# Two gathers in flight, each begun on the landing of the last but one, in both edge walks of a graph layer with routed experts

## The reference, cut to what matters

```
# graph attention, 8 heads of 32
q, k, v = x @ Wq + bq, x @ Wk + bk, x @ Wv + bv
logits  = einsum('ehd,ehd->eh', q[dst], k[src]) / sqrt(32)
expv    = exp(logits - segment_max(logits, dst)[dst])
attn    = expv / segment_sum(expv, dst)[dst]
agg     = segment_sum(attn * v[src], dst)
y       = x + gelu(agg + x @ Wskip + bskip);  layernorm(y) * gamma + beta

# routed experts: a second small attention (4 heads of 4) over 131072 edges
h       = x @ W_gat;  e = leaky_relu(a_src[src] + a_dst[dst]);  alpha = softmax of e per dst
scores  = mean over heads of layernorm(segment_sum(h[src] * alpha, dst) + b_gat)
out     = sum over 4 experts of gate * (gelu(x @ W1 + b1) @ W2 + b2)     # top 2 of 4 by scores
```

## Time and profile before

| | us |
|---|---|
| median of 3 runs | 4069.05 (4067.04 to 4070.93) |
| span of the profiled execution | 5874.6 |
| first to last gather of attention | 339.6 to 3494.4 |
| first to last gather of routing | 3740.4 to 5692.5 |
| GpSimd busy | 2589.4 |
| VectorE busy | 3464.7 |
| TensorE busy with matmuls | 3912.2 |
| GpSimd waiting for the message step (attention) | 1232.4 |
| GpSimd waiting for a free routing slot | 675.7 |

### The profile page before, as it was taken

One profiled execution on the slowest core, in us unless ns is written; L12 is line 12 of the kernel. 1 busy time (PEld: TensorE's weight loads), 2 busy tenths in 40 slices (PEclk: granted clock), 3 DMA queues, 4 the chain that ended last, 5 costly groups with the idle time before them and its releaser, 6 DMA issues. The chain is left out here.

```text
span 5874.6 us, 106076 instructions
## 1 busy us (share of the span) xinstructions
PE 3912.2 (67%) x26108; PEld 2753.9 (47%) x26109; DVE 3464.7 (59%) x9273; ACT 2543.2 (43%) x6305; POOL 2589.4 (44%) x2723
## 2 busy tenths in 40 slices
PE   7857777777777777777777773355666666666550
PEld 3335555555555556555555563233434343443330
DVE  8856666666666666666666668434444444444348
ACT  4445555555555555554555555223333333333320
POOL 3244444444444444444445441444444444445540
PEclk9978888888888888888888885577877787777765
DMA  6455555555555555555556555111111111111117
GB/s 212 147 163 165 155 168 163 163 161 168 156 159 163 161 168 156 165 158 165 154 166 172 159 150 177 44 15 18 21 19 21 19 21 19 22 18 19 20 21 263
DMA packets 367690, 683.50 MB, mean 116 GB/s; under 512 B 70294, under 2 KB 240482, under 8 KB 367074
## 3 DMA queue, kind: packets, MB, share of 16 engines
q0 software_dynamic: 157888, 427.05, 27.9%
q1 hardware_dynamic: 183106, 223.68, 11.5%
q10 hardware_dynamic: 26080, 25.70, 1.5%
HBM read 588.41 MB, written 87.78 MB: 115 GB/s over the span
## 5 line engine op out<-in xcount | busy, mean ns | idle before, releaser
L746 POOL DMA_INDIRECT KV<-kv_d,src_i x1564 | 1482.7, 948 | 1677.7 <-DVE msg L839 1232.4
L1389 POOL DMA_INDIRECT re_src<-src_tab_d,rsrc x1024 | 974.5, 952 | 978.7 <-SPq L1399 675.7
L1013 PE MATMUL agg_ps<-msg,oh 128*128 128x264 f32 x3512 | 1085.8, 455 | 229.7 <-issue 218.4
L1013 PEld LDWEIGHTS agg_ps<-msg,oh 128*128 128x128 f32 x3512 | 744.4, 222 | 414.2 <-issue 282.7
L1597 PE MATMUL ex_y_ps<-ex_w,ex_hid 128*112 128x256 f32 x1792 | 586.6, 461 | 301.6 <-issue 299.1
L966 PE MATMUL Q<-q,ohT 128*128 128x256 bf16 x5328 | 753.0, 297 | 15.6 <-issue 13.9
L839 DVE TENSOR_TENSOR msg<-KV,weigh_ps 128x1056 f32<-128x1056 f32 x439 | 545.7, 1243 | 268.6 <-ACT weigh_ps L920 250.1
L1516 ACT COPY re_ohT<-re_ohT_ps 128x1024 bf16<-128x1024 bf16 x179 | 181.0, 1011 | 1075.0 <-remote 1010.6
L966 PEld LDWEIGHTS Q<-q,ohT 128*128 128x128 bf16 x5328 | 531.4, 105 | 117.4 <-issue 19.5
L909 ACT ACTIVATE square<-iota_b,off 128x128 bf16<-128x128 bf16 x1784 | 569.2, 392 | 0.3
L1597 PEld LDWEIGHTS ex_y_ps<-ex_w,ex_hid 128*112 128x112 f32 x1792 | 363.7, 214 | 434.1 <-issue 366.0
(11 more groups left out here) (264 smaller groups left out, 6199.0 us busy)
## 6 DMA issues: line engine op xcount, KB each, us to landing
q<-q_d SPq DMA_DIRECT2D x446, 192.0 KB
y_d<-ex_y ACTq DMA_DIRECT2D x56, 448.0 KB
rg_ye<-y_d SPq DMA_DIRECT2D x7, 3584.0 KB, 11.8
KV<-kv_d,src_i POOLq DMA_INDIRECT x1564
nu_xs<-xs_d SPq DMA_DIRECT2D x7, 2688.0 KB, 11.9
re_src<-src_tab_d,rsrc POOLq DMA_INDIRECT x1024
kv_d<-pr_kv SPq DMA_DIRECT2D x49, 260.0 KB, 2.2
xs_d<-pr_xs SPq DMA_DIRECT2D x49, 256.0 KB, 2.4
```

The costliest lines, as they stand in the source:

```text
L746: pool.indirect_dma_start(out=KV[:, t % (KVR * G), :], out_offset=None, in_=k.kv_d, in_offset=bass.IndirectOffsetOnAxis(ap=k.src_i[:, t:t ...
L1013: m = pe.matmul(agg_ps[:, 0:HEADS * HW], oh32[ring(s, 2)][:, t, :], msg[ring(s, 2)][:, t, :, :].rearrange("p h e -> p (h e)"), start=False ...
L1389: pool.indirect_dma_start(out=gs[:, t % (RING * RG), :], out_offset=None, in_=k.src_tab_d, in_offset=bass.IndirectOffsetOnAxis(ap=k.rsrc[: ...
```

## The change

Both walks now hold at most two gathers in flight: before gather t, GpSimd waits for the landing of gather t-2 (`FLY = 2`). Semaphores count by tile in place of group or half group. A group's tiles are announced when its last gather has landed. In the routing walk GpSimd makes this announcement, and SyncE keeps only the release of slots. What else is computed and moved stays as it was.

```diff
+FLY = 2
 ...
 # attend
-        kv_landed = [nc.alloc_semaphore(f"at_kv_landed{i}") for i in range(4)]
+        kv_landed = [nc.alloc_semaphore(f"at_kv_landed{i}") for i in range(G)]
 ...
-                def landed(n):
-                    pool.wait_ge(kv_landed[n % 4], 16 * G * (n // 4 + 1))
-                    pool.sem_inc(ok["tiles"], G)
+                def landed(t):
+                    pool.wait_ge(kv_landed[t % G], 16 * (t // G + 1))
+                    if t % G == G - 1:
+                        pool.sem_inc(ok["tiles"], G)
 ...
                     for t in range(n * G, (n + 1) * G):
+                        if t >= FLY:
+                            landed(t - FLY)
                         pool.indirect_dma_start(...)
-                                                ).then_inc(kv_landed[n % 4], 16)
-                    if n:
-                        landed(n - 1)
-                landed(NG - 1)
+                                                ).then_inc(kv_landed[t % G], 16)
+                for t in range(NT - FLY, NT):
+                    landed(t)
 ...
 # route_experts
+                def landed(t):
+                    pool.wait_ge(gathered[t % 4], 16 * (t // 4 + 1))
+                    if t % RG == RG - 1:
+                        pool.sem_inc(ok["tiles"], RG)
                 for n in range(RNG):
                     if n >= RING:
                         pool.wait_ge(ok["used"], n - RING + 1)
-                    for half in range(2):
-                        h = 2 * n + half
-                        if n:
-                            pool.wait_ge(gathered[(h - 2) % 4], 16 * (RG // 2) * ((h - 2) // 4 + 1))
-                            pool.sem_inc(ok["ring_seen"], 1)
-                        for t in range(n * RG + half * (RG // 2), n * RG + (half + 1) * (RG // 2)):
-                            pool.indirect_dma_start(...).then_inc(gathered[h % 4], 16)
+                    for t in range(n * RG, (n + 1) * RG):
+                        if t >= FLY:
+                            landed(t - FLY)
+                        pool.indirect_dma_start(...).then_inc(gathered[t % 4], 16)
+                for t in range(RT - FLY, RT):
+                    landed(t)
 ...
             def _(sp):
-                for n in range(RNG):
-                    if RING <= n + RLEAD < RNG:
-                        old = n + RLEAD - RING
-                        end = sp.value_load(k.rlast_tab[0:1, old:old + 1], min_val=1, max_val=RSTEPS)
-                        sp.wait_ge(ok["val"], end)
-                        sp.sem_inc(ok["used"], 1)
-                    for h in (2 * n, 2 * n + 1):
-                        sp.wait_ge(gathered[h % 4], 16 * (RG // 2) * (h // 4 + 1))
-                    sp.sem_inc(ok["tiles"], RG)
+                for n in range(RING, RNG):
+                    end = sp.value_load(k.rlast_tab[0:1, n - RING:n - RING + 1], min_val=1, max_val=RSTEPS)
+                    sp.wait_ge(ok["val"], end)
+                    sp.sem_inc(ok["used"], 1)
```

More of the change, by code:

```diff
@@ L1382, in _ @@
                         pool.wait_ge(ok["used"], n - RING + 1)
-                    for half in range(2):
-                        h = 2 * n + half
-                        if n:
-                            pool.wait_ge(gathered[(h - 2) % 4], 16 * (RG // 2) * ((h - 2) // 4 + 1))
-                            pool.sem_inc(ok["ring_seen"], 1)
-                        for t in range(n * RG + half * (RG // 2), n * RG + (half + 1) * (RG // 2)):
-                            pool.indirect_dma_start(out=gs[:, t % (RING * RG), :], out_offset=None, in_=k.src_tab_d,
-                                                    in_offset=bass.IndirectOffsetOnAxis(ap=k.rsrc[:, t:t + 1], axis=0)).then_inc(gathered[h % 4], 16)
+                    for t in range(n * RG, (n + 1) * RG):
+                        if t >= FLY:
+                            landed(t - FLY)
+                        pool.indirect_dma_start(out=gs[:, t % (RING * RG), :], out_offset=None, in_=k.src_tab_d,
+                                                in_offset=bass.IndirectOffsetOnAxis(ap=k.rsrc[:, t:t + 1], axis=0)).then_inc(gathered[t % 4], 16)
+                for t in range(RT - FLY, RT):
+                    landed(t)
             @block.sync
             def _(sp):
-                for n in range(RNG):
-                    if RING <= n + RLEAD < RNG:
-                        old = n + RLEAD - RING
-                        end = sp.value_load(k.rlast_tab[0:1, old:old + 1], min_val=1, max_val=RSTEPS)
-                        sp.wait_ge(ok["val"], end)
-                        sp.sem_inc(ok["used"], 1)
-                    for h in (2 * n, 2 * n + 1):
-                        sp.wait_ge(gathered[h % 4], 16 * (RG // 2) * (h // 4 + 1))
-                    sp.sem_inc(ok["tiles"], RG)
+                for n in range(RING, RNG):
+                    end = sp.value_load(k.rlast_tab[0:1, n - RING:n - RING + 1], min_val=1, max_val=RSTEPS)
+                    sp.wait_ge(ok["val"], end)
+                    sp.sem_inc(ok["used"], 1)
             @block.vector
```

## The result

The change takes 5479.6 us (median of 4 runs, 5474.4 to 5485.1) against 4068.1 us (4067.0 to 4070.9): ratio 1.347, 95% interval 1.345 to 1.349. The forecast was 5,575 us, in a range of 4,700 to 5,930.

The account below looks back on a forecast made before the run. Timed runs were taken to go at, or within about 2% of, GpSimd's gather rate. With two in flight, 767.7 outside the walks + 3269 attention + 1536 routing = 5573 us; forecast 5,575 us, 37% slower, range 4,700 to 5,930.

Parts of the forecast that it names:

- main case: Both walks: two gathers in flight make landing plus start the limit; 5,575 us, own range 5,350 to 5,800, chance 53%.
- outside the walks: Time before, between and after the two walks' gathers, taken from the first profiled execution and kept unchanged: 767.7 us.
- attention, 1564 gathers: Attention walk: cycle of 4.19 us shared by two gathers, 2.09 us each, 3269 us in all.
- routing, 1024 gathers: Routing walk: cycle of 2.99 us shared by two gathers, 1.50 us each, 1536 us in all.
- The cycle: Both walks: mean distance of gather starts is half of landing plus next start, or 1.252 us where that is longer.
- Landing: Gather's start to its landing: 3.4 us in attention, 2.2 in routing, each including 0.1 from closing packet to semaphore.
- Landing to start: GpSimd, from a landing to the start of the gather it releases: 0.79 us in both walks, bounds 0 and 0.85.
- Rival A: Landing without other traffic is faster, 2.7 us in attention and 2.1 in routing: 4,985 us, chance 22%.
- Rival B: The 0.79 us start is hidden, prepared during the wait; routing at the bare 1.252 us: 4,709 us, chance 11%.
- Rival C: Faster: fewer gathers crowd code and query loads less and TensorE's issue pauses go; 4,008 us at best, chance 3%.
- Rival D: Limit doesn't bind in timed runs: start under 0.4 us, landing 2.1 in both walks; 4,069 us, chance 3%.
- Rival E: Distances between gathers at their upper bounds, 2.32 us in attention and 1.53 in routing: 5,963 us or more, chance 8%.

Follow-up runs that it names:

- the increment kernel: The change with an increment of an unused semaphore behind every other landing wait too, so an instruction stands between each wait and gather: 5911.5 us, ratio 1.4523.

## Why the prediction was right, and where it was not

Side, mechanism and size were right: 5479.6 us lies in the main case, 5,350 to 5,800, and the sum gave 5573 us for a span of 5472.8. That it came within 2% is in part luck, as two terms were off in opposite directions. By its own terms, on the kernel after:

| term | forecast | measured |
|---|---|---|
| outside the walks | 767.7 | 717.3 |
| attention, 1564 gathers | 3269 (2.09 us) | 3192.9 (2.04 us) |
| routing, 1024 gathers | 1536 (1.50 us) | 1562.6 (1.53 us) |

- *The cycle.* Landing plus start, divided by the number in flight, holds in both walks and with five in flight; with three its landing had to be another one.
- *Landing.* 3.4 and 2.2 us were put, medians of 3.4 and 2.4 were measured. The 0.1 us in both from closing packet to semaphore was an estimate without a row: the trace has 0.34 (median; mean 0.38), which is all that routing's landing lacked. In attention a closing packet at 3.15 us for the 3.3 that was put made up for it. But a chain pays the mean, and the means (of the gathers whose landings can be matched) are 3.53 and 2.53 us; one in nine of attention's and one in five of routing's took over 15% more than the median.
- *Landing to start.* This is the mis-sized term. I took 0.79 us for every gather from the earlier trace rows, where in truth an instruction with a wait and an increment stood ahead of the gather in both rows. Only one gather in four of attention has that after the change; two begin 0.26 us after the landing, and the fourth is held by GpSimd's own 1.25 us behind the late one. Over the matched gathers of attention, the odd chain, the mean is 0.56: 3.53 + 0.56 = 4.09, twice the measured 2.04, as it must be by the way the two are defined; it is not a second proof. So landing too short by 0.13 and start too long by 0.23 partly cancelled. In routing 2.2 + 0.79 stood for a landing of 2.53 and the 0.53 that is left of twice 1.53, and there they cancelled almost wholly. Bounded "from 0 to 0.85", the term was inside.
- *Rival A* (shorter landing without traffic) needed 2.7 us; the median landing was 3.4. *Rival B* (hidden start) was half right: where the gather carries its own wait, 0.26 us is left of the 0.79. Its time was not, since it needed all of it hidden, 1.25 us a gather in routing where 1.53 was measured, and the increment kernel shows what brings the 0.78 back. *Rival C*: nothing got faster outside the cycle; -12.9 us outside the walks is all. *Rival D* (the limit doesn't bind): GpSimd waited 1552 and 457 us for landings. *Rival E*: its bound was reached in routing, 1.53 us, and not in attention, 2.04 us for 2.32; it needed both.
- *Outside the walks*, 50 us too much was carried over from the stretched execution.
- *What bounds attention before* was VectorE and not in part the gathers: the message distance of 4.65 us gave 2041 us, measured 2044.5. It did not change the sum, because after the change only the gather's cycle counts; it would have, had the distance of two starts come out at 1.3 us.
- *The profiled execution.* I forecast some 6,050 us for the span after, with a wait for the message step of a few hundred us, and said the change would nearly be hidden there. That was wrong, 5472.8 and 4.7: the lateness of the consumers was not the kernel's under a profiler, it was that one execution's, and never came back in eleven further profiles. The inference that the timed runs hold none of it was right.

No version here beats the kernel before. Attention is at VectorE's pace there and routing at GpSimd's rate of issue, and nothing done to the number in flight touches either; five in flight is its equal.

## What to carry to other kernels

A ring of DMAs with n in flight costs (start to landing + landing to next start)/n each, or the issue's own time if that is longer. Find the n at which the second is the longer, with the mean landing at that depth, and keep one more: here two cost 35%, three 10%, four 0.7%, five nothing. If something has to stand between a wait and a DMA's start, put it behind the start: ahead of it the increment made this start 0.52 us later here, behind it not, though only 0.20 us a group of four came back in time. When a profile's span is far from the timed median, profile again before reading waits from it; lower bounds (bare rate times count plus what lies outside) can still be trusted, and gave the right side here.

## What the runs showed of the hardware

- A gather on GpSimd that carries its own wait began 0.26 us after the landing; with a wait-and-increment instruction between them 0.78 us after (medians over 391 and 390 gathers of attention).
- The same code had a profiled execution of 5874.6 us and one of 4070.6 us. In the first TensorE paused for "issue"; in the second it was busy 1907 of 1980 us in attention. What stretched it no run shows.
- With gathers spaced out, TensorE's granted clock fell: in attention's window before it was 1.00, the 2.4 GHz level throughout, with TensorE busy 96% of the time; after, 0.87, a mean over stretches at 2.4 and at 1.2 GHz, with TensorE idle for 889 us while it waits for VectorE's running maxima, which wait for the gathers. The windows of the kernel after, to compare with those of the kernel before above:

```profile
400.00:3520.00 3120.00, 2255.72 (x17649) 1788.38 (x17648) 2004.86 (x4301) 1665.31 (x4733) 1443.56 (x1528) 0.87 0.57 161
...
3770.00:5320.00 1550.00, 1071.39 (x6877) 690.77 (x6873) 835.25 (x3722) 633.80 (x792) 972.41 (x1016) 0.86 0.15 24
```

TensorE is the busiest engine there by this account, but its matmuls took 2256 us for 1907 in about as many instructions. That the clock is on no path that ends last is read from who waits for whom: VectorE's product waits 1097 us for announcements, and none of its large waits is for TensorE.

The Trainium skill, page "DMA: Bandwidth & Descriptors", section "Anatomy of one DMA — SWDGE (gpsimd) path", puts a fixed part of 2.0 us into such a DMA and adds its bytes at 436 GB/s. By that formula, an estimate from the page, the routing gather of 10 KB comes to 2.0 us and the attention gather of 266 KB to 2.6. The trace of the change has 2.4 and 3.4 from start to landing (medians), more than the page in both.
